# Decoder layer with a sparse expert stage: expert tiles brought in by transposing DMA, attention outputs turned by TensorE, scatters of the third block in fours

## The reference

```python
x = layernorm(x + favor_attention(x))       # 16 heads of 64, 128 features, causal, linear
x = layernorm(x + cross_attention(ctx, x))  # 77 context rows, 2 x 16 half heads, differential
x = layernorm(x + moe(x))

qp = exp(q @ W_feat - |q|^2 / 2) / sqrt(128)            # the same for keys
S_t = S_{t-1} + k_t v_t^T ; z_t = z_{t-1} + k_t ; y_t = (q_t S_t) / (q_t z_t + eps) ; y @ Wo

# moe: 16 experts (256 -> 128 -> 256), 4 per token out of 2 of 4 groups, plus a shared expert
inter = silu(x @ gate_e.T) * (x @ up_e.T) ; expert_e = inter @ down_e.T
out = sum over the 4 chosen of weight * expert_e + shared(x)
```

## Time and profile before

| | us |
|---|---|
| median of 3 runs (lowest, highest) | 821.26 (818.77, 822.57) |
| the profiled execution | 822.12 |
| its span, first to last instruction | 820.4 |
| PE busy, share, instructions | 743.9, 91%, 9512 |
| DVE busy | 508.2, 62% |
| ACT busy | 431.9, 53% |
| POOL busy | 290.3, 35% |
| mean granted TensorE clock | 0.963 |

### The profile page before, as it was taken

One profiled execution on the slowest core, in us unless ns is written; L12 is line 12 of the kernel. 1 busy time (PEld: TensorE's weight loads), 2 busy tenths in 40 slices (PEclk: granted clock), 3 DMA queues, 4 the chain that ended last, 5 costly groups with the idle time before them and its releaser, 6 DMA issues.

```text
span 820.4 us, 24197 instructions
## 1 busy us (share of the span) xinstructions
PE 743.9 (91%) x9512; PEld 512.0 (62%) x9512; DVE 508.2 (62%) x1511; ACT 431.9 (53%) x889; POOL 290.3 (35%) x346
## 2 busy tenths in 40 slices
PE   8999999999999998799999879986588996998975
PEld 4666677567766765476676446665466774764543
DVE  5877663693576686247748643574477445743686
ACT  7888773657564453566536346420255753644232
POOL 5421211123312034434101463205234354436862
PEclk9999999999999999899999998999699998899997
DMA  8347557485375267557803531475135323313542
GB/s 283 140 136 208 158 155 174 136 248 159 117 205 155 98 193 209 161 136 191 267 10 88 143 121 35 175 207 170 59 104 150 105 87 120 120 71 119 165 159 98
DMA packets 123389, 119.58 MB, mean 146 GB/s; under 512 B 55440, under 2 KB 110864, under 8 KB 122768
## 3 DMA queue, kind: packets, MB, share of 16 engines
q1 hardware_dynamic: 116624, 101.52, 42.6%
q0 software_dynamic: 5376, 15.47, 5.0%
q10 hardware_dynamic: 1280, 1.05, 0.5%
HBM read 42.65 MB, written 66.97 MB: 134 GB/s over the span
## 4 chain that ended last, share of the span: by engine, by line
PE 68%; DVE 13%; another core or an unknown queue 8%; ACT 5%; issue 4%; DMA 1%; POOL 1%; ACTq 0%; SPq 0%; DVEq 0%
PE ps L1806 26%; PE ps L1814 17%; PE ps L1930 8%; PE ps L1911 3%; PE ps L1946 3%; PE ps L2056 3%; DVE xmax L1650 1%; PE ps L1947 1%; PE ps L2041 1%; PE ps L2148 1%; DVE st L1434 1%; DVE attn_mem L1616 1%; DMA xq<-wk 1%; PE ps L1976 1%
## 5 line engine op out<-in xcount | busy, mean ns | idle before, releaser
L1050 POOL TENSOR_TENSOR qk<-square,qk 128x512 f16<-128x512 f32 x64 | 74.6, 1166 | 146.3 <-ACT qk L1153 146.2
L1814 PE MATMUL ps<-attn_mem 128*64 128x65 f32 x1920 | 96.0, 228 | 4.6 <-issue 3.5
L1814 PEld LDWEIGHTS ps<-attn_mem 128*64 128x64 f32 x1920 | 80.8, 140 | 24.7 <-issue 22.7
L1806 PE MATMUL ps<-x_split,w_qkv 128*128 128x512 f16 x384 | 93.5, 381 | 0.3 <-DVE qk L1612 0.3
L1054 POOL TENSOR_TENSOR yT<-y,yT 128x512 f16<-128x512 f32 x20 | 23.1, 1156 | 197.2 <-ACT yT L1171 197.2
L1078 POOL DMA_INDIRECT rows_out<-attn_mem,dest x64 | 61.8, 965 | 85.9 <-ACT attn_mem L1262 67.1
L1199 ACT ACTIVATE prob<-ps 128x512 f32<-128x512 f32 x96 | 53.3, 605 | 34.3 <-PE ps L2056 15.0
L1156 ACT ACTIVATE attn_mem<-ps 128x512 f32<-128x512 f32 x64 | 34.8, 595 | 59.5 <-PE ps L1911 59.5
L1806 PEld LDWEIGHTS ps<-x_split,w_qkv 128*128 128x128 f16 x384 | 36.7, 98 | 41.7 <-issue 3.9
L1071 POOL DMA_INDIRECT rows_in<-rows,slot_i x48 | 46.5, 968 | 38.4 <-DVE slot_i L1545 25.2
L1814 PEld LDWEIGHTS ps<-xv,prob 128*64 128x64 f32 x1536 | 49.4, 139 | 16.6 <-issue 12.8
(11 more groups left out here) (319 smaller groups left out, 1898.5 us busy)
## 6 DMA issues: line engine op xcount, KB each, us to landing
rows_in<-zero_row SPq DMA_DIRECT2D x32, 576.0 KB, 4.3
rows_in<-zero_row SPq DMA_DIRECT2D x16, 720.0 KB
attn_mem<-rows_in SPq DMA_DIRECT2D x64, 144.0 KB
late_mem<-ffn_w SPq DMA_DIRECT2D x17, 384.0 KB, 3.5
y_parts<-yT SPq DMA_DIRECT2D x40, 128.0 KB
up_split<-late_mem SPq DMA_DIRECT2D x16, 256.0 KB, 3.6
rows_in<-zero_row SPq DMA_DIRECT2D x16, 144.0 KB
down_split<-late_mem SPq DMA_DIRECT2D x16, 128.0 KB, 3.9
```

The lines of the kernel that those rows point to most:

```text
L1050: pool.tensor_tensor(parts[:, 3, :], square[:, n % 2, :], parts[:, 2, :], ALU.subtract).then_inc(p_sql.sem, 1)
L1806: ins = pe.matmul(dst, lhs(i), rhs(j), start=first and n == 0, stop=last and n == 2)
L1814: ins = pe.matmul(dst[at:at + COLS, :], lhs[:, at:at + COLS], rhs, start=start, stop=stop)
```

## The change

All of it is one edit of the program:

- **Attention outputs.** All 32 pairs are turned by TensorE, as the 12 were. The 20 splits on POOL, the 40 stores and the 20 transposing DMAs of y are gone, and so are the 14 matmuls on zeros.
- **Expert tiles.** A new job "rows" splits a block's normed rows once: ACT writes the high part (128x1024), POOL the low part, as fp16 halves of one row of 1152 bytes, now in the last 1152 columns of the `prob` ring. The scatter sends those rows. A tile then comes in by one transposing DMA on SP (128 rows of 512 fp16) straight into the form that PE multiplies; the 128 transposes, the 32 splits on ACT and the 32 on DVE are gone. The ring is still of 8 pairs; the first two lie in `x_stage`, and may be loaded before the last block's attention is done.
- **Weights and destinations.** They come by a small DMA per tile (128x32 float32) of their own, issued by ACT after the pair's activation behind the up product (64 DMAs), and are waited for at "tile down".
- **Waits.** The job that writes the probabilities of chunk 3 of a block waits until the block before has all 16 scatters landed, since rows lie there; a block's first scatter waits for "rows"; the load of x waits for "rows" where it waited for the scatters.
- **Scatters of the third block.** They wait, each four, until all issued before have landed.
- **The tables** are retuned throughout, of which two entries: CHAIN has `dispatch=22.694` and `dispatch_d=0.476` (was 25.666 and 0.159), CHAIN_2 `dispatch=20.861` and `dispatch_d=0.065` (was 17.18 and 0.001).

The diff, cut to its core:

```diff
+ROW_RING = (RING * TB - NT * RW) // TB
...
-STANDS = 14
-DIRECT = tuple((b, n) for b in range(NBLK) for n in range(PAIRS) if b == 0 or b >= DENSE - 1 and n >= PAIRS - 2)
...
-            if (b, n) in DIRECT:
-                put(H * b + 2 * n + ATT["turn_output"], "turn output", b, n)
-            else:
-                ends = "_last" if n == PAIRS - 1 else ""
-                put(H * b + 2 * n + ATT["send" + ends], "send output", b, n)
-                put(H * b + 2 * n + ATT["take" + ends], "take output", b, n)
+            put(H * b + 2 * n + ATT["turn_output"], "turn output", b, n)
...
+        put(start + at["rows"], "rows", b, 0)
...
-        row_mem = sb("rows", [P, 2, NT, RW])
-        stream = row_mem[:, :, :, 0:D]
+        stream = sb("stream", [P, 2, NT, D])
...
+        row_mem = prob_mem[:, RING * TB - NT * RW:RING * TB].rearrange("p (t c) -> p t c", t=NT)
+        row_parts = [row_mem[:, :, D // 2 * a:D // 2 * (a + 1)].bitcast(F16) for a in range(2)]
...
-        xg = carve(attn_mem, at, XG * 2 * RW).rearrange("p (r j c) -> p r j c", r=XG, j=2)
-        xgT = carve(attn_mem, at, 3 * 2 * KD * P).bitcast(F16).rearrange("p (r a t) -> p r a t", r=3, a=2)
+        xr = carve(attn_mem, at, 3 * 2 * 2 * NE).rearrange("p (r j c) -> p r j c", r=3, j=2)
+        xgT = [m.bitcast(F16).rearrange("p (j q t) -> p j q t", j=2, q=2 * KD)
+               for m in [x_stage[:, k, :] for k in range(KD)] + [carve(attn_mem, at, 2 * KD * P) for _ in range(XG - KD)]]
...
-                    sp.wait_ge(*yt_sent(0, sent(b, n + 1)))
-                    for a in range(2):
-                        sp.dma_start(y_scr[PAIRS * b + n, :, a, :].rearrange("(c p) d -> p c d", p=P),
-                                     yT[:, a, n, :].rearrange("p (c d) -> p c d", c=NT)).then_inc(y_stored.sem, 16)
-                elif kind == "take output":
-                    sp.wait_ge(*y_stored(0, 2 * sent(b, n + 1)))
-                    sp.dma_start_transpose(yT[:, :, n, :], y_scr[PAIRS * b + n, :, :, :].rearrange("t a d -> t (a d)")
-                                           ).then_inc(yt_loaded.sem, 16)
...
-                        sp.wait_ge(*scattered[b - 2](0, NT * TOPK))
+                        sp.wait_ge(*row_low(b - 2, 1))
...
+                        sp.wait_ge(*summed(NBLK - 2, 2))
+                        sp.dma_start(sum_scr[NBLK - 2], acc[:, :, :]).then_inc(sum_stored.sem, 16)
...
                     if i == 0:
+                        sp.wait_ge(*x_low(NBLK - 1, 1))
+                    if i == 2:
                         sp.wait_ge(*o_done(NBLK - 1, H))
...
-                        sp.dma_start(xg[:, i % XG, j, :], rows_in[b][bass.ds(row, P), :]
-                                     ).then_inc(xg_loaded[i % XG].sem, 16)
+                        sp.dma_start_transpose(xgT[i % XG][:, j, :, :], rows_in[b].bitcast(F16)[bass.ds(row, P), 0:2 * D]
+                                               ).then_inc(xg_loaded[i % XG].sem, 16)
...
-                    pool.wait_ge(*yt_high(b, n + 1))
-                    pool.tensor_tensor(yT[:, 1, n, :], y[:, n % 2, :, :].rearrange("p c d -> p (c d)"), yT[:, 0, n, :],
-                                       ALU.subtract).then_inc(yt_sent.sem, 1)
...
+                elif kind == "rows":
+                    pool.wait_ge(*row_high(b, 1))
+                    pool.tensor_tensor(row_parts[1], stream[:, b % 2, :, :], row_parts[0], ALU.subtract
+                                       ).then_inc(row_low.sem, 1)
...
+                        pool.wait_ge(*row_low(b, 1))
                         pool.wait_ge(*slots_ready(b, 1))
                         i = GROUPS[0].index(b)
                         pool.wait_ge(*cleared[i](0, NE if i + 1 < len(GROUPS[0]) else NE + SPARE[0]))
+                    elif b == NBLK - 2 and n % 4 == 0:
+                        pool.wait_ge(*scattered[b](0, n))
                     pool.indirect_dma_start(
                         rows_in[GROUP_OF[b]], bass.IndirectOffsetOnAxis(ap=slot_i[:, b, n:n + 1], axis=0),
-                        row_mem[:, b % 2, n // TOPK, :], None).then_inc(scattered[b].sem, 16)
+                        row_mem[:, n // TOPK, :], None).then_inc(scattered[b].sem, 16)
...
+                elif kind == "turn output":
+                    act.wait_ge(*yt_done(b, n + 1))
...
+                    if b and n == ROW_RING:
+                        act.wait_ge(*scattered[b - 1](0, NT * TOPK))
...
-                elif kind == "tile turn":
-                    i = pair_id(b, n)
-                    act.wait_ge(*t_turned(0, i + 1))
-                    if i >= 3:
-                        act.wait_ge(*t_up(0, i - 2))
-                    act.activation(xgT[:, i % 3, 0, :], bank[:, :], ACT.Copy).then_inc(t_high.sem, 1)
+                elif kind == "rows":
+                    act.wait_ge(*normed[1](b, NT))
+                    act.activation(row_parts[0], stream[:, b % 2, :, :], ACT.Copy).then_inc(row_high.sem, 1)
...
+                        act.dma_start(xr[:, i % 3, j, :], rows_in[b][bass.ds(row, P), D:RW]
+                                      ).then_inc(xr_loaded[i % 3].sem, 16)
...
+                    act.wait_ge(*xr_loaded[i % 3](i // 3 + 1, 0))
                     for j in range(2):
                         m = (2 * n + j) % LOADED
                         e = experts[m // PER_E] // 16 ** (m % PER_E) % 16
-                        act.activation(dest[:, i % YB, j:j + 1], xg[:, i % XG, j, bass.ds(e + (D + NE), 1)], ACT.Copy)
+                        act.activation(dest[:, i % YB, j:j + 1], xr[:, i % 3, j, bass.ds(e + NE, 1)], ACT.Copy)
                         last = act.activation(yb[:, i % YB, j, :], bank[:, D * j:D * j + D], ACT.Copy,
-                                              scale=xg[:, i % XG, j, bass.ds(e + D, 1)])
+                                              scale=xr[:, i % 3, j, bass.ds(e, 1)])
...
-                    if (b, n) == (NBLK - 1, PAIRS - 1):
-                        stand(bank)
...
-                            last = pe.transpose(bank[:, P * m:P * m + P], xg[:, i % XG, j, P * k:P * k + P], ident[:, :])
-                            address_ahead()
-                    last.then_inc(t_turned.sem, 1)
-                    free[index] = [t_high(0, i + 1), t_low(0, i + 1)]
...
+                    pe.wait_ge(*xg_loaded[i % XG](i // XG + 1, 0))
```

More of the change, by code:

```diff
@@ L127 @@
[L127 to L129 removed]
+ATT = dict(project=(-2.354, -1.694), turn_keys=(2.063, 2.138), q_features=0.932, k_features=0.936,
+           attend=(1.748, 3.734), state=(2.675, 3.719), output=(3.721, 4.674), turn_output=5.451, values_0=2.306,
+           values_1=1.187)
@@ new lines @@
+CHAIN = dict(rows=16.754, first=3.463, first_d=0.503, out=3.839, out_d=0.116, norm1=4.752, turn=5.182, queries=5.488,
+             scores=6.998, scores_d=0.072, maxima=9.671, probs=9.857, probs_d=0.122, norm2=12.552, cross=15.313,
+             gate=15.91, route0=15.644, up=16.766, route1=16.295, route2=17.769, down=17.91, route3=18.563,
+             prefix=19.074, dispatch=22.694, keep=26.299, table=21.385, dispatch_d=0.476)
+CHAIN_2 = dict(rows=19.556, first=2.996, first_d=0.794, out=3.978, out_d=0.067, norm1=4.744, turn=5.144,
+               queries=5.562, scores=6.742, scores_d=0.076, maxima=9.676, probs=10.123, probs_d=0.129, norm2=13.13,
+               cross=15.291, gate=17.004, route0=16.474, up=18.026, route1=17.809, route2=18.86, down=20.687,
+               route3=20.136, prefix=20.354, dispatch=20.861, keep=21.975, table=20.954, dispatch_d=0.065)
@@ L132, in schedule @@
+MISC = dict(ctx_out=14.344, ctx_out_d=1.575, clear_d=0.469, values=3.27, values_d=0.335, split=0.877, split_d=0.176,
+            context=1.668, keys=-1.194, tail=9.61, setup=2.817, setup_d=0.961, load_x=-3.493, split_x=-2.516,
+            load_stream=0.611, experts_0=-4.69, experts_1=-4.284, rows_in=-9.613, up=1.838, down=4.264)
 def schedule():
@@ L196, in schedule @@
     return [(when, job) for when, _, job in sorted(jobs)]
-def sent(b, n):
-    return sum((i, k) not in DIRECT for i in range(NBLK) for k in range(PAIRS) if (i, k) < (b, n))
 def chain_jobs(put, start, b, at):
@@ L310 @@
            "project first", "project out", "turn stream", "queries", "scores", "turn maxima", "probs", "weigh", "turn cross", "gate",
-           "shared up", "shared down", "prefix", "pack", "weights", "tile turn", "tile up", "tile down", "dense gate",
+           "shared up", "shared down", "prefix", "pack", "weights", "tile up", "tile down", "dense gate",
            "dense up", "dense weigh")
```

137 lines of the change are left out of this document (52 added, 85 removed).

## The result

| | before | after |
|---|---|---|
| median, us (range, runs) | 820.01 (817.68 to 822.57, 4) | 780.64 (779.5 to 784.16, 4) |
| ratio, 95% interval | | 0.9526 (0.9482 to 0.9571) |
| profiled execution, its span | 822.12, 820.4 | 781.03, 779.3 |
| mean granted TensorE clock | 0.963 | 0.968 |

The change takes 39 us off; the forecast was 24.6, to 797.5, with a range down to 782. The direction was right and the size was not. Later runs on other chips changed what this number means: see the later groups of experiments.

The account below looks back on a forecast made before the run. TensorE (PE), busy 91% of the span, was taken as the bound, with idle time where POOL scatters. Terms -20.5 + 12.8 - 3.2 - 11.7 - 9 + 6 + 1 = -24.6 took 822.1 to 797.5 us; range 782 to 824.

Parts of the forecast that it names:

- rival A: PE's gaps at the scatters don't hang on scatter run length; those terms fall away, sum -3.9, 818 us; chance 0.17.
- third block's fours: Stretch 565 to 590 us loses 17.7; four runs of four would still lose 6, so -11.7 us (0 to -13).
- scatters of blocks 0 and 1: Two stretches, 305 to 345 and 454 to 499 us, lose 23.3; shorter runs were taken to save 9 (0 to -17.4).
- all the rest: Tile transposes gone -20.5, output transposes added +12.8, matmuls on zeros gone -3.2, longer pair latency +6, rows' split +1.
- first six microseconds: In the third block's scatter run, PE stays full for the first six or so microseconds and is starved after.
- The term of the load on ACT: Tile stage: ACT gains 64 issues of 618 ns, 39.6 us; longer pair latency costs PE +6 us (0 to +12).
- Rival B: Tile stage: PE waits for ACT's two DMA issues per pair, up to 40 us in place of +6, 831 us; chance 0.18.
- The waits of the fours: On POOL, the third block's last scatter leaves after some 33 us, which just fits; nothing taken, 10 us as a case.
- Rival C: Third block's pauses exceed a landing and tiles' outputs wait behind them: +10 to +15, 808 to 812 us; chance 0.10.
- dips at blocks 0 and 1: Sign of a right forecast: PE's dips in busy time near the scatters of blocks 0 and 1 halve.
- picture of the third stretch: Sign, 560 to 590 us: PE idles in four short pieces of 1 to 2 us after scatter groups, clock over 0.9.
- The matmuls on zeros: On PE, 14 matmuls ahead of a turn, 3.2 us, are removed: -3.2 us (0 to -4.6).

Follow-up runs that it names:

- b_spread: Kernel before with scatters of blocks 0 and 1 spread (dispatch_d 0.159 to 0.32), on a chip of 822 us: 804.1 us, ratio 0.9778.
- b_fours: Kernel before with the third block's scatters in fours, each waiting for those before, on a chip of 822 us: 810.2 us, ratio 0.9878.
- a_sixteen: Changed kernel without the waits between the third block's scatters: 794.1 us, 0.9670 of the kernel before; repeated (_2) on a 747 us chip: 743.86 us, 0.9958.
- a_bunched: Changed kernel with scatters of blocks 0 and 1 in one run of sixteen each: 806.5 us, 0.9823 of the kernel before (822 us chip).
- b_sf_3: Kernel before with scatters of blocks 0 and 1 spread and the third block's in fours, where the kernel before takes 819.67 us: 791.91 us, ratio 0.9652.
- a_xrdouble: Changed kernel with each small DMA on ACT's queue issued twice, on a 747 us chip: 767.15 us, 1.0268 of the kernel before.

## Why the prediction was right or wrong

**The bound** was read rightly: PE, with its idle time where POOL scatters. **The mechanism** was too: on chips of this kind long runs of scatters starve PE's issue, and rival A (the gaps do not hang on the length of the runs; the sum then 818) fell with b_spread, b_fours, a_sixteen and a_bunched. That the fetch of instructions is what starves was argued from the earlier trace rows and is shown by no run. If it is, the Trainium skill's "mostly hidden" (Runtime: NRT & Kernel Launch, section Instruction fetch mechanics) fits the chips of 747 us, 3.7 us of idle time by issue in all, and not those of 821 us, 39.2.

**The sum**, term by term, on chips that take about 821 us:

| step | forecast | measured | by |
|---|---|---|---|
| third block's fours | -11.7 | -10 (-6 to -14) | b_fours; +12 where a_sixteen undoes it |
| scatters of blocks 0 and 1 | -9 | -18 (-15 to -22) | b_spread |
| all the rest (-20.5 + 12.8 - 3.2 + 6 + 1) | -3.9 | -10 (-6 to -15) | after less b_sf_3 (38.9 - 28.5) |
| sum | -24.6 | -39 | |

The step that failed is the term of the scatters of blocks 0 and 1: "I take -9; the bounds are 0 and -17.4". The stretches had lost 23.3, and I gave most of that to busy DMA engines. b_spread shows 18 of it to be starvation, and a_bunched shows PE starved at a DMA share of 0.33. The price was there to be taken: in the third stretch the same scatters cost 17.7, and I had claimed that the first six microseconds are free; runs of at most three then cost nothing. Even my bound of 17.4 was tight: the clock had stayed at 0.92 from 340 to 360 us, beyond the first window. That is 9 of the 14 us.

The second part is the rest, -10 for -3.9. It holds the change's own spread of the scatters too, which leaves 3.4 us of idle time in the stretches of blocks 0 and 1 where b_spread leaves 6.3, so some 3 us of it belong to the term above. Its turns cost what was forecast as busy time (12.1 for 12.8). On the other kind of chip the same parts, without the waits, give -3 (a_sixteen_2, 0.0042 x 747), so the sum of the work terms was right where nothing starves, and the rest of the -10 appears only where something does. Fewer instructions of PE in the tile stage, whose transposes had 6.7 us of idle time by issue, are a likely cause; it was not isolated.

**The term of the load on ACT**, +6 with issues of 618 ns: an issue takes 340, and taking all 64 away gains 4, which is not told apart from nothing. Rival B was priced with the wrong duration and did not happen; twice the number of issues (a_xrdouble) costs 15 us.

**The waits of the fours**, taken at nothing: about 8 us where the chip does not starve PE. Where it does, their cost was not measured apart from what they bring; that both together came out near the -11.7 is in part luck. Rival C's mechanism is real (12.5 us of ACT waiting for output buffers), but it did not decide the time that was forecast: there the first output scatter went 27.8 us after the first of the third block's scatters (570.36 less 542.55), not over 45.

**The signs.** Two of the forecast's held: the dips at blocks 0 and 1 more than halved, and the 128 turns take 155 ns each. The picture of the third stretch did not hold in the changed kernel: it still idles 12.7 us of 40 at a clock of 0.79, where four short pieces and a clock over 0.9 were forecast. The forecast had left out that the turn of the normed stream must wait for norm 1 there, and that output scatters would follow the last four and lengthen the run to eight. In b_fours, whose outputs come 4.1 us after the last of the fours, the clock does stay at 1.00 from 560 to 600 us.

**The matmuls on zeros** were not tried alone. The turns without retuned tables cost 27 to 28 and not 9.6: the price per instruction was right (12.1 and -3.0 for 12.8 and -3.2), the idle time behind them (9.7) and the longer time of other groups (4.7) were left out of the sum. The changed kernel does not show such a cost; that its tables avoid it is a guess.

What the prediction could not see is that its largest terms belong to a kind of chip. One profile, of one chip, stood behind it.

## What to carry to other kernels

Where TensorE idles with no semaphore to blame and another engine issues indirect DMAs at that moment, count the run: on the chips that show it, three in a row cost almost nothing and sixteen cost 14 us, rows of 128 bytes starve it as rows of 1152 do, and a due time in a table mends it. Look too at what follows the last of a broken run. Before such a gain is built on, time both kernels on a second chip: here 39 us on one kind are a loss of 5 on the other. A wait that is put in to break such a run belongs where nothing is queued behind it; the best version on the chips of 747 us is the changed kernel without the fours (743.9 against 747.4), on those of 821 us the one with them (780.6; 778.1 with SP's loads, not told apart).

## What the runs showed of the hardware

- Chips differ by kind: two took 745 to 747 us in the median for the kernel before, two 820 to 822, and none of its executions lay between 751 and 816. The chip of the first comparison, at 820, behaved as the latter. What differs between them was not found. Two of the four were used a second time, four and seven minutes after the first, and kept their kind; whether it is the chip itself or something else that stays so long (where the program or its data lie in memory, other work on the machine) no run separates.
- On the second kind, runs of indirect scatters on POOL keep PE from issuing: one instruction or a few per 0.7 to 2 us, no semaphore in between, and the granted clock falls to the lower level (0.50 from 442 to 449 us in a_bunched). Which part of the chip is short was not found. Rows of 128 bytes do it as well as rows of 1152. On the first kind sixteen in a row leave PE busy 18.7 of 21 us.
- A DMA of 128 rows of 32 float32 took ACT 340 ns to issue in the median, against 618 for the ones of 64 KB in the earlier trace rows; waiting for the landing of four scatters took POOL 1.7 to 3.4 us beyond the last of them (b_fours, after).
